# A twelve-sublayer decoder: ten stages as one block, with another order at each stage's beginning

## What is computed

```python
x = _layernorm(x + _L0_attn_ref(x, ...))
x = _layernorm(x + _L0_xattn_ref(x, ctx_768, ...))
x = _layernorm(x + _L0_ffn_ref(x, ...))
...
x = _layernorm(x + _L3_attn_ref(x, ...))
x = _layernorm(x + _L3_xattn_ref(x, ctx_768, ...))
x = _layernorm(x + _L3_ffn_ref(x, ...))
```

## Time and profile before

| | us |
|---|---|
| median of three runs | 3370.93 |
| lowest and highest of them | 3364.6 to 3373.39 |
| profiled execution | 3366.96 |
| its span (first to last instruction in the trace) | 3364.7 |
| PE busy in the span | 3081.5 (92%) |
| VectorE, ScalarE, GpSimd busy | 1882.7, 1716.8, 1531.7 |
| mean granted TensorE clock | 0.962 |

### The profile page before, as it was taken

The page is one execution under the profiler, slowest core; times in us unless marked ns, Lnnn a source line. Parts: engine busy times, 40 slices in busy tenths (PEclk is TensorE's granted clock), DMA queues, the critical chain, the costliest instruction groups (busy, mean ns, idle before and its releaser), DMA issues. The chain is left out here.

```text
span 3364.7 us, 60083 instructions
## 1 busy us (share of the span) xinstructions
PE 3081.5 (92%) x23977; PEld 2613.8 (78%) x23977; DVE 1882.7 (56%) x3913; ACT 1716.8 (51%) x3727; POOL 1531.7 (46%) x1165
## 2 busy tenths in 40 slices
PE   6997999999798898898997989799997999979997
PEld 5676888888676566898665877678886888879997
DVE  4764222222566465686553764467765666655555
ACT  4763333332266554564664653356665666535555
POOL 0123344434212775586234551133334444439996
PEclk8998999999899999899997999899999999999999
DMA  1002000100000010342001000110001000026673
GB/s 66 3 12 78 22 20 19 38 1 1 23 3 23 1 51 1 127 177 94 3 3 44 9 34 18 39 51 1 1 1 38 5 6 4 1 87 222 221 220 98
DMA packets 49827, 156.98 MB, mean 47 GB/s; under 512 B 9338, under 2 KB 29470, under 8 KB 37136
## 3 DMA queue, kind: packets, MB, share of 16 engines
q1 hardware_dynamic: 45808, 142.91, 12.3%
q0 software_dynamic: 3744, 10.23, 1.0%
HBM read 142.07 MB, written 10.26 MB: 45 GB/s over the span
## 5 line engine op out<-in xcount | busy, mean ns | idle before, releaser
L1304 POOL TENSOR_TENSOR prob<-prob,inv 128x512 f32<-128x512 f32 x320 | 331.3, 1040 | 401.7 <-DVE inv L1356 392.4
L1194 ACT ACTIVATE prob<-banks,nmax 128x256 f32<-128x256 f32 x640 | 296.7, 473 | 154.1 <-DVE nmax L1350 154.0
L2683 POOL TENSOR_TENSOR hL<-product,hH 128x512 fp32r<-128x512 f32 x128 | 165.7, 1294 | 321.2 <-ACT hH L2630 321.2
L2728 DVE TENSOR_TENSOR product<-banks,silu 128x512 f32<-128x512 f32 x128 | 88.6, 692 | 388.1 <-PE banks L2554 332.8
L2289 DVE TENSOR_REDUCE nmax<-banks 128x4 f32<-128x1024 f32 (+1 forms) x192 | 217.5, 1133 | 151.2 <-PE banks L1871 83.4
L2622 ACT ACTIVATE silu<-banks 128x512 f32<-128x512 f32 x128 | 76.5, 598 | 367.5 <-PE banks L2554 367.3
L1350 DVE TENSOR_REDUCE nmax<-banks 128x2 f32<-128x512 f32 x320 | 215.3, 685 | 20.5 <-PE banks L1173 16.1
L2554 PE MATMUL banks<-xH,upH 128*128 128x512 f32 x512 | 201.9, 394 | 5.8 <-POOL upL L2670 5.8
L2554 PE MATMUL banks<-xL,upH 128*128 128x512 f32 x512 | 201.5, 394 | 0.0
L2554 PE MATMUL banks<-xH,upL 128*128 128x512 f32 x512 | 199.7, 390 | 0.0
L1094 PE MATMUL bank<-ident,prob 128*128 128x128 f32 x1280 | 166.7, 273 | 6.3 <-POOL prob L1304 6.3
(11 more groups left out here) (622 smaller groups left out, 11024.0 us busy)
## 6 DMA issues: line engine op xcount, KB each, us to landing
W<-in_L_ffn_experts SPq DMA_DIRECT2D x80, 1024.0 KB, 6.1
W<-in_L_ffn_experts SPq DMA_DIRECT2D x8, 1536.0 KB, 8.0
slots_y<-W SPq DMA_DIRECT2D x23, 256.0 KB, 6.2
W<-strips SPq DMA_DIRECT2D x4, 768.0 KB, 7.4
W<-in_L_ffn_experts SPq DMA_DIRECT2D x9, 256.0 KB, 4.7
X<-in_x SPq DMA_DIRECT2D x1, 2048.0 KB, 8.4
cs<-in_ctxT SPq DMA_DIRECT2D x16, 128.0 KB, 2.3
W<-in_L_ffn_experts SPq DMA_DIRECT2D x1, 2048.0 KB, 7.8
```

Of the source, the lines that this page charges most:

```text
L1194: ins = nc.scalar.activation(m_.prob[p % 2][:, e * 512 + j * S:e * 512 + (j + 1) * S], bank(key)[:, j * S:(j + 1) * S], ACT.Exp, bias=m_.n ...
L1304: nc.gpsimd.tensor_tensor(pr, pr, m_.inv[:, slot(p, e):slot(p, e) + 2].unsqueeze(2).to_broadcast([P, 2, S]), ALU.mult)\
L2683: nc.gpsimd.tensor_tensor(m_.hL[:, at], m_.product[s % 2][:, :], m_.hH[:, at].bitcast(F32), ALU.subtract).then_inc(g.h_low.sem, 1)
L2728: nc.vector.tensor_tensor(m_.product[s % 2][:, :], bank(("u", s))[:, :], m_.silu[s % 2][:, :], ALU.mult)\
```

## The change

1. **One block.** A class `Stage` takes the place of `nc.Block()` for the stages: it only records the five parts. At the end of `decoder` one `nc.Block()` runs for each engine the parts of all stages one after the other (`in_turn`). The barriers between the stages are gone; the one behind the set-up stays. The parts of GpSimd and VectorE hold `yield` marks that `in_turn` passes over: both complete a stage, then begin the next.

2. **Waits instead of barriers.** ScalarE, GpSimd, SP and in `attention16` VectorE begin a stage with `products_done`: the last bank of the stage before must be filled. PE waits before each transpose of X until the last stage has written that batch (`x_from`), SP before it prefetches the weights of the stage after or stores X.

3. **Other orders at the beginnings.** L0_ffn splits expert 0's up weights in four pieces by output column, high and low, and PE waits for each piece only when it needs it. `attention16` splits q's and k's weights and transposed batch 0 before v's weights, and makes the bias product after the first transposes. L2_ffn and L3_ffn split the gate first, transpose and multiply with it for three quarters of X, and take the last quarter after; L3_ffn also has its first up weights in four pieces, and its fills of constants after them. GpSimd clears all 128 rows of the context's padding in `attention64` instead of 64, and no longer waits for itself. L2_attn keeps its residual in a part of the weight buffer.

```diff
+class Stage:
...
+    def __exit__(self, *_):
+        self.bases = [s.base for s in self.g.signals]
+        self.g.stages.append(self)
...
+def in_turn(stages, part_of, eng):
+
+    for stage in stages:
+        stage.recall()
+        for _ in part_of(stage)(eng) or ():
+            pass
+
+
+def products_done(eng, g, last):
+
+    if last is not None:
+        eng.wait_ge(g.filled[last].sem, g.filled[last].base)
...
-    with nc.Block() as block:
+    last_bank, x_from, ready = g.last_bank, g.x_from, Ready(g.x_done, 1)
+
+    with Stage(g) as block:
...
             def transpose_x(b):
+                x_from.wait(pe, b)
...
             wait_weights(act, g, n)
+            products_done(act, g, last_bank)
             for part, j in pieces[0:2]:
...
         def _(pool):
+            products_done(pool, g, last_bank)
             if ctx:
-
                 for cs in m_.cs:
-                    nc.gpsimd.memset(cs[C - P:P, S:2 * S], 0.0).then_inc(g.ctx_padded.sem, 1)
-                pool.wait_ge(g.ctx_padded.sem, g.ctx_padded.base + 2)
+                    nc.gpsimd.memset(cs[:, S:2 * S], 0.0).then_inc(g.ctx_padded.sem, 1)
...
         wait_weights(act, g, n)
+        products_done(act, g, last_bank)
         for part in "qkv":
+            if part == "v":
+                x_high(0)
             nc.scalar.activation(split(m_.wH, part), raw[part], ACT.Copy, scale=0.25 if part == "q" else 1.0).then_inc(g.split_high.sem, 1)
...
         nc.vector.tensor_tensor(split(m_.wL, "k"), raw["k"], split(m_.wH, "k").bitcast(F32), ALU.subtract).then_inc(g.scaled.sem, 1)
+        x_low(0)
+        if bias:
+            filled(dve, "bias")
...
-                if c == 0 and f == 0:
-                    up_pieces(pe, e)
+                if c == 0:
+                    up_pieces(pe, e, f)
...
+            first_up_high(0)
             x_high(0)
-            up_high(0)
+            for f in range(1, 4):
+                first_up_high(f)
             x_high(1)
...
-            for q in range(4):
-                up_piece(0, q)
+            products_done(pool, g, last_bank)
+            up_piece(0, 0)
+            yield
+            for f in range(1, 4):
+                up_piece(0, f)
...
+            for c in range(PAIRS - 1):
+                transpose_x(c)
+            pe.wait_ge(g.w_split.sem, g.w_split.base + 1)
+            for c in range(PAIRS - 1):
+                logits_of(c)
+            transpose_x(PAIRS - 1)
             up_of(0)
+            logits_of(PAIRS - 1)
+            up_of(1)
...
-    with nc.Block() as block:
+    with Stage(g) as block:
...
+        with nc.Block() as block:
...
+            @block.gpsimd
+            def _(pool):
+                in_turn(g.stages, lambda stage: stage.pool, pool)
+
+            @block.vector
+            def _(dve):
+                in_turn(g.stages, lambda stage: stage.dve, dve)
```

More of the change, by code:

```diff
@@ L355, in follow, with staged, run @@
             pass
-def run(nc, shared, programs, order):
+def staged(parts, order, tail):
+    for at, k in enumerate(order):
+        if at == 1:
+            yield
+        if at == tail:
+            yield
+        next(parts[k], None)
+    for part in parts:
+        for _ in part:
+            pass
+    if tail is None:
+        yield
+def run(g, shared, programs, order, last, pool_tail, dve_tail):
     follow([p.places() for p in programs], order)
-    with nc.Block() as block:
+    with Stage(g) as block:
         @block.sync
@@ L1630, in places @@
                 misc(("xT", t))
+                if t == 0 and bias:
+                    misc("bias")
             for j in range(2):
@@ L1893, in tensor @@
                 done(("xT", t), mm)
+                if t == 0 and bias:
+                    offsets()
             for j in range(2):
@@ L3290, in sources, with transpose_x @@
                 done("source", mm)
-            for c in range(PAIRS):
+            def transpose_x(c):
+                x_from.wait(pe, 2 * c + 1)
                 for k in range(2):
@@ L3606, in find_tokens, with x_low @@
                 step(nc.vector.tensor_tensor(w2, ex, w1, ALU.mult))
[L3608 removed]
+            def x_low(c):
                 for k in range(2):
@@ L3875, in _ @@
                     .then_inc(g.freed[u.bank(("lg", c))].sem, 1)
+            wait_weights(act, g, n)
+            products_done(act, g, last_bank)
+            nc.scalar.activation(m_.gateH[:, :], gate, ACT.Copy).then_inc(g.w_high.sem, 1)
+            x_high(0)
+            high(SHARED)
+            x_high(1)
+            x_high(2)
+            for c in range(PAIRS - 1):
+                logits_out(c)
+            x_high(PAIRS - 1)
+            logits_out(PAIRS - 1)
             high(0)
```

366 lines of the change are left out of this document (256 added, 110 removed).

## The result

| | before | changed |
|---|---|---|
| median of the runs, us | 3369.71 (4 runs, 3364.6 to 3373.39) | 3346.05 (4 runs, 3343.84 to 3347.59) |
| ratio, 95% interval | | 0.993 (0.9913 to 0.9948) |
| span of the profiled execution | 3364.7 | 3343.3 |
| mean granted TensorE clock | 0.962 | 0.966 |

A forecast was written before the change was run, and what follows sets the result against it. PE, busy 3081.5 of 3364.7 us, was taken as the bound, so gain could come only from its 283 us idle. The boundary terms sum to 19.7 us: 3347.3 from the profiled execution, 3351.2 from the median; forecast 3348, range 3334 to 3360.

The forecast's parts named there:

- L0_ffn, 6.4 forecast: L0_attn to L0_ffn: upL starts during the tail, PE needs one piece, X's writes alternate with GpSimd's; 6.4 us (0.7 to 8.3).
- L1_attn, 4.1: L0_ffn to L1_attn: q and k split during the tail, bias and masks behind xTL; gain 4.1 us (0 to 7.9).
- L2_ffn, 2.5: L2_xattn to L2_ffn: 24 of 32 transposes leave the path, 4.1 less 1.6 for lower clock; 2.5 us (1 to 4.5).
- L3_attn, 0.2: L2_ffn to L3_attn: X's four writes alternate with GpSimd's weight splits, strip copy behind; 0.2 us (−0.5 to 4.4).
- L3_xattn, 1.0: L3_attn to L3_xattn: GpSimd's clearing of cs no longer stands 1.03 us behind the barrier; 1.0 us (0.5 to 1.5).
- L3_ffn, 2.5: L3_xattn to L3_ffn: 24 of 32 transposes leave the path, 4.3 less 1.6 for lower clock; 2.5 us (1 to 4.5).
- Set-up, 1.1: Set-up to L0_attn: 1.0 of blocking beside a GpSimd fill avoided, 0.1 for V's high half; 1.1 us (0 to 1.7).
- That L314 passes beside GpSimd: Rival at the boundaries: VectorE's writes of X run unblocked beside GpSimd; gain 30.5 us, so 3337; chance 0.2.
- That GpSimd keeps its turn: Rival at the boundaries: held writes of X wait until GpSimd runs out of work; gain 9.7, so 3357.3; chance 0.13.
- The slower case: Rival in the bulk: fewer rests lower PE's granted clock; 0.01 costs 32 us, giving 3379; chance 0.05.
- The heads do start early: Denies the rival that a new wait holds the heads as long as the barrier did: 3362, chance 0.05.
- a head's gain that returns further on: Sign of error: gain returns as a wait, in L0_ffn for upL pieces 1 to 3, in L1_attn for the masks.

The follow-up runs named there:

- e4_late_transposes: Changed kernel, but in L2_ffn and L3_ffn the tensor engine makes its first transpose only when all of X is written; 3351.79 us.
- e2_gpsimd_waits: Changed kernel, but GpSimd begins next-stage work at L0_ffn, L1_attn, L2_attn (behind two fills) and L3_attn only when X is written; 3343.97 us, ratio to before 0.9922.
- e5_fills_later: e2_gpsimd_waits, but L1_attn's four 128x1024 fills come behind VectorE's work on by_slot; 3339.89 us, ratio to before 0.99.
- e7_four_pieces: Changed kernel, but in L0_ffn the tensor engine waits for all four pieces of expert 0's upL before its first product; one run, 3351.58 us.
- e1_barriers: Changed kernel, but each stage is its own block again with the barrier behind it; new orders and waits stay; 3362.89 us, ratio to before 0.9978.

## Why the prediction was right, step by step

*L0_ffn, 6.4 forecast.* 6.5 and 5.5 in the two traces at the first `product`, and 6.40 in both at TensorE's first matmul. The walk with its alternating instructions was right to 0.1 us. It did not say that the pieces or the early start alone would have made nearly all of it.

*L1_attn, 4.1.* 3.8 and 4.1, with the fills pushing the tail (its first write took 2.19 us) and a cast of 3.85 or 2.07 us beside fills; the first `qkL` had gained 5.3 and 6.0, and 1.5 to 1.9 went back until the second.

*L1_ffn 1.0, L2_attn 0.6, L2_xattn 0.3.* 1.1, 0.9 and nothing that repeats.

*L2_ffn, 2.5.* 3.2. The mechanism was the right one (`e4_late_transposes`, 3.1), and so was the 1.6 us for a restart at a lower clock: the first 18 products with the gate took 1.5 us more than before.

*L3_attn, 0.2.* 0.4 and 1.1; the strip copy itself came 0.6 earlier. Right, as was its upper end of 4.4 without the blocking: with `e2_gpsimd_waits` the copy comes 4.5 earlier.

*L3_xattn, 1.0.* The step that failed. The head gained the barrier and more (1.4), as forecast, but the term took the clock behind it to be the same. It was lower in both traces of the changed kernel, and 0.7 to 1.2 us were lost in all. Where it was not lower (`e5_fills_later`, `e7_four_pieces`), 2.0 and 1.6 were gained.

*L3_ffn, 2.5.* 0.7 and 0.9. (Its terms, 4.3 less 1.6, give 2.7.) The head gained 3.0, with the forecast's 1.6 already paid in the products with the gate. What the forecast set at nothing is that another 2.2 went back behind the token logits. The new order puts 36 of the first 48 up products ahead of them, so that fewer are left for TensorE while VectorE picks the experts. That it is the order and not the missing barrier is shown by `e1_barriers`, which has the order alone, the same clock of 0.68 there, and +3.47.

*Set-up, 1.1.* Not to be seen in the table: L0_attn spreads by 7.7 us over the eleven traces of changed kernels (+2.79 to −4.95), and the two traces of before by 2.2. The means of the two groups, −2.2 and −1.1, are as far apart as the forecast says, which beside this spread shows nothing.

Added up over the boundaries in the table, with the longer of two rows where there are two, the two traces of the changed kernel have 15.9 and 15.5 us against the 18.6 of the forecast without the set-up. So the terms were 3 us too high together, by the last two. The measured 23.7 were 4 above the forecast all the same: the rest lies in stretches that the change leaves alone, and depends on the runs. The first pair of traces is 21.4 apart, the second 12.7, the two times on the second chip 19.1. How much of what goes beyond the 15 us and the set-up belongs to the change stays open. That the forecast of 3348 lies only 2 us from the measured 3346.05 is therefore partly luck: the terms came out lower, stretches nobody touched added to them, and the forecast was laid nearer to the profiled execution, where the same sum from the median gave 3351.2.

*The rivals.* That L314 passes beside GpSimd fell with 2.62 and 5.28 us. That GpSimd keeps its turn fell with the same rows for subtractions, but is what the fills do in part of the traces, and moving them gained 2 to 3 us at the first `qkL` of L1_attn. (The 9.5 us that this rival counts for the other boundaries are 8.4 in the sum of the first rival, so its time should have been some 1 us later.) The slower case fell: the mean clock was 0.966 for 0.962. The heads do start early. TensorE's busy time moved by 3.6 us, within the 5 allowed, and eight transposes are left behind the gate's first products at L2_ffn and L3_ffn. What the prediction named as a sign against it, a head's gain that returns further on, came at L3_ffn, but by the clock and not as a wait.

## What to carry to other kernels

Where engines meet at a barrier, cutting the first weights so that the first product needs a quarter of them, and starting them during the tail of the stage before, are largely one gain; do the simpler. Of work moved beside a tail, look at who writes the last result: if VectorE, let GpSimd wait for it, and keep bursts of fills out of the way of any cast or scaling on the path. Here the two together gave 6 to 10 us by the times, beside some 20 for the whole change, and by the traces 1.9 at L0_ffn, 3.9 at L3_attn's strip and 2.2 to 2.9 at L1_attn. And take a second trace before explaining a difference in a stretch that nobody touched.

## What the runs showed of the hardware

A write of X (`TENSOR_SCALAR`, 128x256) beside GpSimd's subtractions got in between each two of them (2.62 us for 0.73, 5.28 for 1.38). Beside fills (`MEMSET`, 128x1024, 0.95 us each) it often did not: 2.19 us behind two, a cast 3.85 us behind four, 4.64 behind a subtraction and four. In four traces the same cast beside the same four fills took 2.07 us and got in behind the second. `qkL`, which reads PSUM and SBUF, ran beside the same four fills in 0.88 us. What decides whether a seam between fills is open was not tried.

The Trainium skill, in "SBUF — State Buffer", section "Who interferes with whom", calls the port pair that VectorE and GpSimd share an exclusive lock. The traces agree as far as one GpSimd instruction goes (2.62 us for two writes beside two subtractions); that VectorE is kept out over two fills or four (2.07, 2.19 and 3.85 us) is more than it says.

TensorE's granted clock in one and the same stretch of one and the same program was 0.93 or 0.87, 1.00 or 0.96, from one execution to the next; L0_attn alone spread by 7.7 us over traces of kernels that are alike in it. 18 transposes of no use in one pause, which ended 0.1 us before the next products, held 1.00 for 0.93 and saved 3.1 us; 40 in another pause, which ended 3.6 us before the next products, held 0.95 in the pause and saved nothing: the clock was 0.50 in those products.
